# Values' bias moved into the output's bias, and the copy of the values moved from VectorE to ScalarE

## The chip, the cores and the metric

The kernel runs on one core of a Trainium2 chip. The metric is the device time of one execution in microseconds. TensorE, VectorE, ScalarE, GpSimd and SyncE each work through a program of their own and meet only at semaphores. In the profile they are PE (weight loads: PEld), DVE, ACT, POOL and SP.

## The reference: what is computed

```python
x = L0_attn_x                                  # (2, 2048, 128), float32
x = x + layernorm(attention(layernorm(x)))     # 16 heads of 64
x = x + layernorm(ffn(layernorm(x)))           # rank 32, 512 wide, gelu
# attention:
q, k, v = (einsum('bsd,dhk->bshk', x, W) + b for W, b in ((Wq, bq), (Wk, bk), (Wv, bv)))
attn = softmax(einsum('bqhd,bkhd->bhqk', q / 8, k))
out = einsum('bhqk,bkhd->bqhd', attn, v)
return einsum('bqhd,hdm->bqm', out, Wo) + bo
```

The rows of a softmax add up to 1. So the bias of the values passes through the attention unchanged, and the result equals attention without `bv` plus the constant row sum over h and k of `bv[h,k] * Wo[h,k,m]`.

## The kernel before

The 16 heads are taken as 8 pairs. A pair and one of the 2 batches make a **unit**; there are 16 units, numbered `u` from 0. A unit has 4 **quarters** `c` of 512 queries each, and a quarter has 16 steps, one for each tile of 128 keys. The program takes steps two at a time: a quarter has 8 **double steps** `d`, from 0 to 7, and the kernel has 512 of them, numbered `n`. "The sixth double step" is `d` = 5.

In one double step TensorE does, in this order:

- a pair of products for the row maxima of a later quarter (`max_pair`, L401), one for each head, each into one bank of the spare ring;
- the scores of two steps (L421, L424, L427, two matmuls each, twice), into two score buffers that ScalarE has filled beforehand with the negative maxima ("seeds");
- a second pair of products for maxima (L401);
- what is due in this double step: keys (`project_k`, L369), values (`project_v`, L387: two matmuls of 128 columns for each tile of 128 keys; in the trace every float32 matmul stands as two records, so four for a tile), queries (`project_q`, L378, at `d` = 2), output projection (`out_projection`, L487: 8 matmuls of 128 columns, 16 records, at `d` = 1);
- the products of probabilities and values of the two steps before (`values`, L442);
- at `d` = 3 the sums for the denominators (L454).

The **spare ring** is three banks of PSUM, r0, r1 and r2. The function `spare_banks` walks through the whole program in TensorE's order and gives each use the next bank of the three. `Pe.take` makes TensorE wait until the last user of a bank has been read. Each product for the maxima is reduced by VectorE (`dve_max`, L867).

ScalarE takes the exponentials of the two steps (`act_exp`, L691). In the last double step of a quarter (`d` = 7) its order is: exponential, seed, exponential, seed (`act_seed`, L681). A seed may be written only when the exponential that reads the same score buffer is done, and TensorE's scores of the first two steps of the next quarter wait for their own seed (`seed_done`). ScalarE also copies keys and queries out of PSUM with their biases, and copies the outputs of a quarter (`act_o`, L697).

VectorE does the maxima, four for a double step; the sums over groups of four probability tiles (`dve_part`, L903, at `d` = 3, 5, 6 and 1); the merge of these (`d` = 2); the addition of the output projection into `y_acc` (`dve_y`, L946); and the copy of the values with their bias added (`dve_v`, L858). GpSimd adds up the other part of the probabilities (`pool_add`, L1142), normalises the outputs (L935) and forms the low part of the keys (L1161). SyncE issues the DMAs.

The places of the projections are written out by hand in tables: `V_AT` maps a quarter and a double step of unit `u` to first tile and number of tiles of the values of unit `u + 1`. `FIRST_V_AT` is the same for unit 0. `OWN_V_AT` gives the values of unit 0 itself, in the first three double steps. In all there are 106 groups.

Of the kernel before, what the change touches and what calls it, by code (L numbers as in the profile page):

```python
# [47 lines left out]
V_AT = {(0, 7): (0, 2), (1, 7): (2, 2), (2, 4): (4, 2), (2, 7): (6, 2), (3, 0): (8, 3), (3, 4): (11, 3), (3, 7): (14, 2)}  # L48
# [5 lines left out]
WO_AT = 1  # L54

# [8 lines left out]
FIRST_V_AT = {(2, 7): (0, 4), (3, 0): (4, 4), (3, 4): (8, 4), (3, 7): (12, 4)}  # L64
# [51 lines left out]
def spare_banks():  # L116

    out = {}

    def use(*key):  # L120
        out[key] = f"r{len(out) % 3}"

    for n in range(DOUBLES):
        G, u, c, d = n // PER_CHUNK, n // (PER_CHUNK * NC), n // PER_CHUNK % NC, n % PER_CHUNK
        for st in (2 * n + LEAD, 2 * n + LEAD + 1):
            for h in range(2 if st < STEPS else 0):
                use("max", 2 * st + h)
        if keys_at(u, c, d):
            v, k = keys_at(u, c, d)
            use("K", v * NC + k)  # L130
        if values_at(u, c, d):
            v, t0, nt = values_at(u, c, d)
            use("V", v * T + t0)
        if d == Q_AT and G + 2 < CHUNKS:
            use("Q", G + 2)
        if projected_at(G, d) is not None:
            use("Wo", projected_at(G, d))
        if n in HEADS_AT:
            use("Wo0", HEADS_AT[n])
            use("Wo1", HEADS_AT[n])  # L140
        if n == CENTRE_AT:
            use("U")
        for g in ffn_at(n, XT):
            use("xT", g)
        for g in ffn_at(n, P_AT):
            use("p", g)
        if d == L_AT and 0 < G <= CHUNKS - COLUMN_CHUNKS:
            use("L", G - 1)
        if n in COLUMNS_AT:
            use("L", COLUMNS_AT[n])  # L150
    order = [("xT", 6), ("L", CHUNKS - 1), ("Wo0", CHUNKS - 1), ("Wo1", CHUNKS - 1), ("q", 0), ("p", 6), ("z", 0), ("q", 1), ("z", 1),
             ("q", 2), ("z", 2), ("q", 3), ("xT", 7), ("z", 3), ("p", 7), ("q", 4), ("z", 4), ("q", 5), ("z", 5), ("q", 6), ("z", 6),
             ("q", 7), ("z", 7)]
    for k, key in enumerate(order):
        out[key] = ("r0", "r1", "r2", "o")[k % 4]
    return out
# [5 lines left out]
def build(nc, x, Wq, bq, Wk, bk, Wv, bv, Wo, bo, U1, V1, b1, U2, V2, b2, out):  # L162
# [8 lines left out]
    bv_v = bv.rearrange("(i h) k -> i (h k)", h=2)  # L171

    ctx = ExitStack()
    with ctx:
# [12 lines left out]
        b_v = sb("b_v", [P, 2, P])  # L187
# [48 lines left out]
        def psum(name, shape):  # L236
# [14 lines left out]
            neg_max_done neg_rows_done""".split()  # L251
# [4 lines left out]
        W_DMA_N = 7 * 16  # L256
# [41 lines left out]
        def half(h):  # L298
            return slice(h * HD, (h + 1) * HD)

# [19 lines left out]
        class Pe:  # L320
# [4 lines left out]
            def take(self, name, kind, n):  # L325
# [171 lines left out]

            def centre(self):
# [46 lines left out]
        def pe_program(pe):  # L545
# [26 lines left out]
            for n in range(DOUBLES):  # L572
# [82 lines left out]
        def act_k_high(act, u, c):  # L655
# [5 lines left out]
            nc.scalar.activation(kd_hi[:, u % B, c * CH:(c + 1) * CH], key_diff[:], ACT.Copy).then_inc(s["kd_hi_done"], 1)  # L661

# [93 lines left out]
        def act_program(act):  # L756
# [16 lines left out]
            act_x(act, 4)  # L773
            act_x(act, 5)
# [8 lines left out]
            for n in range(DOUBLES):  # L783
# [6 lines left out]
                if last:  # L790
                    act_seed(act, 2 * n + 3)
                if keys_at(u, c, d):
# [60 lines left out]
        def dve_v(dve, u, t0, nt, name=None):  # L853
            at = u * T + t0
            dve.wait_ge(s["v_ps"], at + nt)
            if u >= 2 and t0 == 0:
                dve.wait_ge(s["pv_done"], (u - 1) * NC * T)
            nc.vector.tensor_tensor(v_sb[:, u % B, t0:t0 + nt, :],  # L858
                                    bank[name or SPARE["V", at]][:, 0:nt * P].rearrange("p (t n) -> p t n", t=nt),
                                    b_v[:, u // B % 2, :].unsqueeze(1).to_broadcast([P, nt, P]), ALU.add).then_inc(s["v_done"], nt)  # L860
# [76 lines left out]
        def dve_y(dve, G):  # L937
# [4 lines left out]
            if G < B * NC:  # L942
                dve.wait_ge(s["bo_in"], 16)
# [102 lines left out]
        def dve_program(dve):  # L1046
            for g in range(NG):
                dve_x_statistics(dve, g)
            for n in range(LEAD):
# [4 lines left out]
                if n == T:  # L1054
                    dve_v(dve, 0, 0, TC, FIRST_V_BANK)
            for n in range(DOUBLES):
# [18 lines left out]
                if values_at(u, c, d):  # L1075
                    dve_v(dve, *values_at(u, c, d))
# [132 lines left out]

        def pool_program(pool):  # L1210
# [33 lines left out]
            first_rstd(7)  # L1244
            for n in range(DOUBLES):
# [32 lines left out]
        def weights(queue, i):  # L1278
# [7 lines left out]
            for dst, src in ((w_qkv[:, j, 1, :], wk_v[i]), (b_qk[:, j, 1:2], bk_v[i].unsqueeze(1)),  # L1286
                             (w_qkv[:, j, 0, :], wq_v[i]), (b_qk[:, j, 0:1], bq_v[i].unsqueeze(1)),
                             (w_qkv[:, j, 2, :], wv_v[i]), (b_v[:, j, :], bv_v[i].partition_broadcast(P)),
# [22 lines left out]
        def sp_denom_back(sp, G):  # L1311
# [3 lines left out]
            if G >= 2:  # L1315
                sp.wait_ge(s["o_norm_done"], G - 1)
            for h in range(2):
# [97 lines left out]
```

## Time and profile before

| | us |
|---|---|
| device time, median of 3 runs | 2386.64 (2386.33 to 2387.66) |
| the profiled execution: its device time | 2388.58 |
| the profiled execution: span from first to last instruction | 2386.7 |
| PE busy in the span | 2348.6 (98%) |
| DVE busy | 2035.4 (85%) |
| ACT busy | 1415.4 (59%) |
| POOL busy | 2107.2 (88%) |
| granted TensorE clock, mean | 0.992 of full speed |

The span is 1.9 us shorter than the device time of the same execution. A timeline row gives start, duration, engine, line of the program, operation, what is written and read, and how many instructions were merged into the row; in brackets stands the idle time before and what ended it. The length of a double step is the distance between the first L421 of one double step and the first L421 of the next.

### The profile page before, as it was taken

Reading aid. Unit: us, or ns where it says so; the run is one execution under the profiler, and the core shown is the slowest. Engines: PE = TensorE matmul, PEld = TensorE weight load, DVE = VectorE, ACT = ScalarE, POOL = GpSimd, SP = SyncE. Lnnn points to the kernel's source line nnn. Section 1 sums busy time; section 2 is a strip of 40 time slices with the busy share of each in tenths; the row PEclk is TensorE's granted clock in tenths of the full one; section 3 lists DMA queues with packets and bytes.
Section 4 is the critical chain, followed back from the end, with each engine's and each line's share of the span. In section 5 each row is a group of like instructions: output and inputs, shape, how many; then the busy total and the mean of one; then the engine's idle time right before and its main releaser. Section 6 shows DMA issues by size and latency. Waiting matters only on the chain.

```text
span 2386.7 us, 43553 instructions
## 1 busy us (share of the span) xinstructions
PE 2348.6 (98%) x15628; PEld 1178.0 (49%) x15628; DVE 2035.4 (85%) x3208; ACT 1415.4 (59%) x1671; POOL 2107.2 (88%) x1206
## 2 busy tenths in 40 slices
PE   6999999999999999999999999999999999999998
PEld 3455454545445454454545445454544545444454
DVE  7888888888888888888888888888888888888877
ACT  5656556566565656656565655656656565655646
POOL 5888989888898989989888898989989888899986
PEclk8999999999999999999999999999999999999999
DMA  1100001000000000100001000100000000110101
GB/s 51 29 14 28 28 15 33 28 15 28 28 20 28 28 15 28 34 15 27 28 16 32 28 19 23 33 23 20 28 27 20 28 28 15 35 30 21 37 27 36
DMA packets 62969, 62.55 MB, mean 26 GB/s; under 512 B 28868, under 2 KB 46660, under 8 KB 62756
## 3 DMA queue, kind: packets, MB, share of 16 engines
q1 hardware_dynamic: 61748, 59.44, 8.5%
q8 instruction: 127, 2.08, 0.4%
q14 instruction: 86, 0.70, 0.1%
q10 hardware_dynamic: 1008, 0.33, 0.1%
HBM read 56.88 MB, written 2.61 MB: 25 GB/s over the span
## 4 chain that ended last, share of the span: by engine, by line
PE 94%; DVE 2%; POOL 1%; DMA 1%; ACT 1%; issue 1%; SPq 0%; POOLq 0%; DVEq 0%; ACTq 0%
PE o_ps L442 37%; PE spare_ps L401 14%; PE score_ps L421 10%; PE score_ps L427 10%; PE score_ps L424 10%; PE spare_ps L387 3%; PE spare_ps L487 3%; PE spare_ps L378 3%; PE spare_ps L369 3%; PE spare_ps L454 1%; DVE max_part L867 1%; POOL total L1142 1%; DMA m_all<-m_scratch 0%; DVE ln_stats L835 0%; PE spare_ps L467 0%
## 5 line engine op out<-in xcount | busy, mean ns | idle before, releaser
L1142 POOL TENSOR_TENSOR total<-total,probs 128x832 f32<-128x832 f32 (+1 forms) x896 | 1761.0, 1965 | 232.6 <-ACT probs L691 161.1
L867 DVE TENSOR_REDUCE max_part<-spare_ps 128x1 f32<-128x512 f32 x2027 | 1303.6, 685 | 295.3 <-PE spare_ps L401 276.7
L691 ACT ACTIVATE probs<-score_ps 128x1024 f32<-128x1024 f32 x1024 | 999.2, 1021 | 785.4 <-PE score_ps L427 784.2
L442 PE MATMUL o_ps<-probs,v_sb 128*64 128x512 f32 x4096 | 977.2, 598 | 0.0
L442 PEld LDWEIGHTS o_ps<-probs,v_sb 128*64 128x64 f32 x4096 | 268.3, 136 | 434.7 <-issue 282.5
L401 PE MATMUL spare_ps<-k_hi,q_hi 64*128 64x512 f32 x2027 | 466.2, 454 | 6.9 <-DVE max_part L867 3.2
L401 PEld LDWEIGHTS spare_ps<-k_hi,q_hi 64*128 64x128 f32 x2027 | 195.2, 184 | 436.8 <-issue 262.1
L421 PE MATMUL score_ps<-q_hi,kd_hi 64*128 64x512 f32 x2048 | 406.9, 393 | 0.9 <-ACT score_ps L681 0.9
L427 PE MATMUL score_ps<-q_hi,kd_lo 64*128 64x512 f32 x2048 | 405.2, 392 | 0.0
L424 PE MATMUL score_ps<-q_lo,kd_hi 64*128 64x512 f32 x2048 | 403.8, 390 | 0.0
L903 DVE TENSOR_REDUCE part_sum<-probs 128x192 f32<-128x768 f32 (+1 forms) x255 | 392.4, 1539 | 0.8 <-ACT probs L691 0.7
L427 PEld LDWEIGHTS score_ps<-q_hi,kd_lo 64*128 64x128 f32 x2048 | 193.2, 185 | 45.2
L424 PEld LDWEIGHTS score_ps<-q_lo,kd_hi 64*128 64x128 f32 x2048 | 193.2, 185 | 42.6
L421 PEld LDWEIGHTS score_ps<-q_hi,kd_hi 64*128 64x128 f32 x2048 | 193.6, 185 | 36.9 <-issue 7.3
L1142 POOL TENSOR_TENSOR total<-probs 128x832 f32<-128x832 f32 x64 | 125.8, 1966 | 14.9 <-ACT probs L691 14.8
L681 ACT ACTIVATE score_ps<-m_all 128x1024 f32<-128x1024 f32 x128 | 131.6, 1029 | 8.0 <-DMA m_all<-m_scratch 4.1
L912 DVE TENSOR_REDUCE total<-part_sum 128x192 f32<-128x768 f32 x64 | 96.9, 1515 | 0.0
L1161 POOL TENSOR_TENSOR kd_lo<-key_diff,kd_hi 128x512 fp32r<-128x512 f32 x64 | 81.7, 1277 | 0.7 <-ACT kd_hi L661 0.7
L387 PE MATMUL spare_ps<-w_qkv,xnT 128*64 128x128 f32 x1008 | 79.0, 285 | 0.4
L935 POOL TENSOR_TENSOR o_sb<-o_sb,denom 128x512 f32<-128x512 f32 x61 | 78.3, 1283 | 0.0
L703 ACT ACTIVATE denom<-spare_ps 128x256 f32<-128x256 f32 x61 | 23.5, 384 | 88.0 <-PE spare_ps L454 88.0
L387 PEld LDWEIGHTS spare_ps<-w_qkv,xnT 128*64 128x64 f32 x1008 | 53.6, 137 | 35.7 <-DVE max_part L867 34.6
(136 smaller groups left out, 1118.5 us busy)
## 6 DMA issues: line engine op xcount, KB each, us to landing
m_all<-m_scratch SPq DMA_DIRECT2D x64, 512.0 KB, 4.4
denom<-denom_scratch SPq DMA_DIRECT2D x122, 128.0 KB, 2.9
m_scratch<-neg_rows SPq DMA_DIRECT2D x256, 1.0 KB
y_acc<-in_L_attn_x SPq DMA_DIRECT2D x8, 256.0 KB, 6.6
key_f<-in_L_attn_x SPq DMA_DIRECT2D x8, 256.0 KB, 2.8
block_out<-probs SPq DMA_DIRECT2D x8, 256.0 KB, 2.3
denom_col<-denom SPq DMA_DIRECT2D x61, 4.0 KB
denom_scratch<-denom_col SPq DMA_DIRECT2D x61, 4.0 KB, 1.4
```

The lines of the kernel that those rows point to most:

```text
L387: last = nc.tensor.matmul(ps[half(k), t * P:(t + 1) * P], xnT[:, at0:at0 + HD], w_qkv[:, slot, 2, :], start=True, stop=True)
L401: last = nc.tensor.matmul(ps[h], q_hi[half(h), G % Q_RING, qt * P:(qt + 1) * P], k_hi[half(h), b, kc * CH:(kc + 1) * CH], start=True, stop ...
L421: nc.tensor.matmul(score_ps[j][:, h, :], kd_hi[half(h), b, keys], q_hi[half(h), G % Q_RING, :], start=False, stop=False, skip_group_check= ...
L424: nc.tensor.matmul(score_ps[j][:, h, :], kd_hi[half(h), b, keys], q_lo[half(h), G % Q_RING, :], start=False, stop=False, skip_group_check= ...
L427: last = nc.tensor.matmul(score_ps[j][:, h, :], kd_lo[half(h), b, keys], q_hi[half(h), G % Q_RING, :], start=False, stop=True, skip_group_ ...
L442: last = nc.tensor.matmul(o_ps[half(h), :], v_sb[:, b, kt, half(h)], probs[:, st % RING, h, :], start=(kt == 0), stop=(kt == T - 1))
L681: nc.scalar.activation(score_ps[st % 2][:], m_all[:], ACT.Copy).then_inc(s["seed_done"], 1)
L691: nc.scalar.activation(probs[:, st % RING], score_ps[st % 2][:], ACT.Exp, scale=SCALE).then_inc(s["exp_done"], 1)
L867: nc.vector.reduce_max(max_part[:, G % 2, h, qt, kc:kc + 1], bank[max_bank(n, h)], AX.X).then_inc(s["max_done"], 1)
L903: nc.vector.tensor_reduce(part_sum[:, k % (T // GROUP), 0:share(G)], probs[:, at:at + GROUP, 0, 0:share(G)].rearrange("p r n -> p n r"), A ...
L912: nc.vector.tensor_reduce(total[:, G % 2, 0, 0:share(G)], part_sum[:, 0:parts, 0:share(G)].rearrange("p g n -> p n g"), AX.X, ALU.add).the ...
L1142: nc.gpsimd.tensor_tensor(others(total[:, G % 2], G), so_far, others(probs[:, st % RING], G), ALU.add).then_inc(s["sum_done"], 1)
```

## The change

The values are projected without a bias. All sixteen tiles of a unit's values are projected in four groups of four tiles, one group at `d` = 5 of each quarter (before: seven groups of two or three tiles, at `d` = 7 of each quarter, `d` = 4 of the third, and `d` = 0 and 4 of the fourth). ScalarE copies each group (`act_v`), after the two exponentials of the double step; VectorE no longer does. The tables for unit 0 are changed too.

The constant row is computed once: two DMAs bring all of `Wo` into the `denom` buffers (unused at that time) and `bv` into a 128 x 8 tile; GpSimd multiplies and adds up over the 8 pairs; in double step 3 TensorE sums over partitions with a matrix of ones (two matmuls of 128 columns, one more use of the spare ring); VectorE adds the result to `bo`. The loads of `bv` with each pair's weights go away (8 DMAs). The first denominators' DMA waits for the read of the `denom` buffers, and the first additions into `y_acc` wait for the summed bias.

```diff
-V_AT = {(0, 7): (0, 2), (1, 7): (2, 2), (2, 4): (4, 2), (2, 7): (6, 2), (3, 0): (8, 3), (3, 4): (11, 3), (3, 7): (14, 2)}
+V_AT = {(0, 5): (0, 4), (1, 5): (4, 4), (2, 5): (8, 4), (3, 5): (12, 4)}
+BIAS_AT = 3
-FIRST_V_AT = {(2, 7): (0, 4), (3, 0): (4, 4), (3, 4): (8, 4), (3, 7): (12, 4)}
+FIRST_V_AT = {(1, 5): (0, 4), (2, 5): (4, 4), (3, 4): (8, 4), (3, 6): (12, 4)}
...
+            def bias(self):
+                self.pe.wait_ge(s["bias_scaled"], 4)
+                ps = self.take(SPARE["bias",], "bias", 0)
+                for k in range(2):
+                    last = nc.tensor.matmul(ps[half(k), 0:D], ones[:], bias_rows[:, 0, :], start=True, stop=True)
+                last.then_inc(s["bias_ps"], 1)
...
+        def act_v(act, u, t0, nt, name=None):
+            at = u * T + t0
+            act.wait_ge(s["v_ps"], at + nt)
+            if u >= 2 and t0 == 0:
+                act.wait_ge(s["pv_done"], (u - 1) * NC * T)
+            nc.scalar.activation(v_sb[:, u % B, t0:t0 + nt, :].rearrange("p t n -> p (t n)"), bank[name or SPARE["V", at]][:, 0:nt * P],
+                                 ACT.Copy).then_inc(s["v_done"], nt)
...
                 act_exp(act, 2 * n + 1)
                 if last:
                     act_seed(act, 2 * n + 3)
+                if values_at(u, c, d):
+                    act_v(act, *values_at(u, c, d))
                 if keys_at(u, c, d):
                     act_k(act, *keys_at(u, c, d))
...
             act_x(act, 4)
+            act_v(act, 0, 0, TC, FIRST_V_BANK)
             act_x(act, 5)
...
-        def dve_v(dve, u, t0, nt, name=None):
-            ...
-            nc.vector.tensor_tensor(v_sb[:, u % B, t0:t0 + nt, :],
-                                    bank[name or SPARE["V", at]][:, 0:nt * P].rearrange("p (t n) -> p t n", t=nt),
-                                    b_v[:, u // B % 2, :].unsqueeze(1).to_broadcast([P, nt, P]), ALU.add).then_inc(s["v_done"], nt)
+        def dve_bias(dve):
+            dve.wait_ge(s["bo_in"], 16)
+            dve.wait_ge(s["bias_ps"], 1)
+            nc.vector.tensor_tensor(bo_sb[:], bank[SPARE["bias",]][:, 0:D], bo_sb[:], ALU.add).then_inc(s["bias_done"], 1)
...
+        def pool_bias(pool):
+            pool.wait_ge(s["bias_in"], 32)
+            nc.gpsimd.tensor_tensor(bias_rows, bias_rows, b_v[:].unsqueeze(2).to_broadcast([P, PAIRS, D]), ALU.mult).then_inc(s["bias_scaled"], 1)
+            for k, count in enumerate((4, 2, 1)):
+                pool.wait_ge(s["bias_scaled"], k + 1)
+                nc.gpsimd.tensor_tensor(bias_rows[:, 0:count, :], bias_rows[:, 0:count, :], bias_rows[:, count:2 * count, :],
+                                        ALU.add).then_inc(s["bias_scaled"], 1)
...
             first_rstd(7)
+            pool_bias(pool)
...
             if G >= 2:
                 sp.wait_ge(s["o_norm_done"], G - 1)
+            elif G == 0:
+                sp.wait_ge(s["bias_ps"], 1)
...
             sp.dma_start(bo_sb[:], bo.partition_broadcast(P)).then_inc(s["bo_in"], 16)
+            sp.dma_start(bias_rows, wo_rows).then_inc(s["bias_in"], 16)
+            sp.dma_start(b_v[:], bv_v, allow_slow_non_contiguous=True).then_inc(s["bias_in"], 16)
             sp_m_out(sp, 0)
```

## Rows read from the trace of the kernel before

**Rows 1.** The page's first part: busy time of each engine, share of the span.

```profile
PE 2348.6 (98%) x15628; PEld 1178.0 (49%) x15628; DVE 2035.4 (85%) x3208; ACT 1415.4 (59%) x1671; POOL 2107.2 (88%) x1206
```

**Rows 2.** Waits: engine, line, releaser: total us, times, longest.

```profile
PEld spare_ps L401 <- DVE max_part L867: 154.5, 284, 2.1
PE score_ps L421 <- ACT score_ps L681: 0.9, 4, 0.3
```

**Rows 3.** TensorE's timeline in unit 6, double step 5 of quarter 0 onwards.

```profile
927.14 0.40 PE L421 MATMUL score_ps<-q_hi,kd_hi 64*128 64x512 f32 x2
...
931.05 0.40 PE L421 MATMUL score_ps<-q_hi,kd_hi 64*128 64x512 f32 x2
...
935.06 0.40 PE L421 MATMUL score_ps<-q_hi,kd_hi 64*128 64x512 f32 x2
...
936.94 0.66 PE L387 MATMUL spare_ps<-w_qkv,xnT 128*64 128x128 f32 x8
...
939.58 0.40 PE L421 MATMUL score_ps<-q_hi,kd_hi 64*128 64x512 f32 x2
...
940.29 0.39 PE L421 MATMUL score_ps<-q_hi,kd_hi 64*128 64x512 f32 x2
...
944.36 0.39 PE L421 MATMUL score_ps<-q_hi,kd_hi 64*128 64x512 f32 x2
...
946.07 1.09 PE L487 MATMUL spare_ps<-w_o,o_sb 128*64 128x128 f32 x16
...
949.15 0.40 PE L421 MATMUL score_ps<-q_hi,kd_hi 64*128 64x512 f32 x2
```

**Rows 4.** VectorE's timeline over the same double steps.

```profile
930.16 1.52 DVE L903 TENSOR_REDUCE part_sum<-probs 128x192 f32<-128x768 f32 x1
931.59 2.66 DVE L867 TENSOR_REDUCE max_part<-spare_ps 128x1 f32<-128x512 f32 x4
```

**Rows 5.** ScalarE's timeline over the same double steps.

```profile
929.87 0.63 ACT L661 ACTIVATE kd_hi<-key_diff 128x512 fp32r<-128x512 f32 x1
931.96 1.94 ACT L691 ACTIVATE probs<-score_ps 128x1024 f32<-128x1024 f32 x2 [1.46 <-PE score_ps L427]
...
937.98 1.01 ACT L691 ACTIVATE probs<-score_ps 128x1024 f32<-128x1024 f32 x1
939.02 1.03 ACT L681 ACTIVATE score_ps<-m_all 128x1024 f32<-128x1024 f32 x1
```

**Rows 6.** TensorE's timeline in unit 0, double step 7 of quarter 0 onwards.

```profile
79.22 0.40 PE L421 MATMUL score_ps<-q_hi,kd_hi 64*128 64x512 f32 x2
...
83.22 0.39 PE L421 MATMUL score_ps<-q_hi,kd_hi 64*128 64x512 f32 x2
...
84.27 0.50 PE L421 MATMUL score_ps<-q_hi,kd_hi 64*128 64x512 f32 x2 [0.19 <-ACT score_ps L681]
...
88.45 0.39 PE L421 MATMUL score_ps<-q_hi,kd_hi 64*128 64x512 f32 x2
```

**Rows 7.** ScalarE's timeline at the same place of unit 0.

```profile
83.19 1.03 ACT L681 ACTIVATE score_ps<-m_all 128x1024 f32<-128x1024 f32 x1
```

**Rows 8.** Groups of instructions by form: count, busy us, mean ns, idle before.

```profile
L697 ACT ACTIVATE o_sb<-o_ps 128x512 f32<-128x512 f32 x64 | 38.3, 599 | 50.0 <-PE o_ps L442 50.0
L935 POOL TENSOR_TENSOR o_sb<-o_sb,denom 128x512 f32<-128x512 f32 x61 | 78.3, 1283 | 0.0
```

**Rows 9.** The start-up, rows of the timeline of SP, PE and POOL.

```profile
38.74 1.59 SPq L1298 DMA_DIRECT2D m_scratch<-neg_rows  x4
...
40.53 0.80 PE L401 MATMUL score_ps<-k_hi,q_hi 64*128 64x512 f32 x2 [0.31 <-DVE v_sb L858]
...
51.46 1.95 POOL L1142 TENSOR_TENSOR total<-probs 128x832 f32<-128x832 f32 x1 [14.64 <-ACT probs L691]
```

**Rows 10.** DMA issues by tile: count, KB each, median us to landing.

```profile
y_acc<-in_L_attn_x SPq DMA_DIRECT2D x8, 256.0 KB, 6.6
b1c<-in_L_ffn_b SPq DMA_DIRECT2D x1, 2.0 KB, 2.4
```

More of the change, by code:

```diff
@@ L137, in spare_banks @@
             use("Wo", projected_at(G, d))
+        if n == BIAS_AT:
+            use("bias")
         if n in HEADS_AT:
@@ L170, in build @@
     bk_v = bk.rearrange("(i h) k -> i (h k)", h=2)
-    bv_v = bv.rearrange("(i h) k -> i (h k)", h=2)
+    bv_v = bv.rearrange("(i h) k -> (h k) i", h=2)
+    wo_rows = Wo.rearrange("(i h) k m -> (h k) i m", h=2)
     ctx = ExitStack()
@@ L186, in build @@
         b_qk = sb("b_qk", [P, 2, 2])
-        b_v = sb("b_v", [P, 2, P])
+        b_v = sb("b_v", [P, PAIRS])
         w_o = sb("w_o", [P, 2, D])
@@ L250, in build @@
             denom_copied col_dma recip_done scratch_dma recip_col_done y_half denom_dma o_copied o_norm_done wo_ps_ready y_done max_ready max_done
-            neg_max_done neg_rows_done""".split()
+            neg_max_done neg_rows_done bias_in bias_scaled bias_ps bias_done""".split()
         s = {n: ctx.enter_context(nc.semaphore(n)) for n in names}
@@ L255, in build @@
         m_dma = [s["m_dma0"], s["m_dma1"]]
-        W_DMA_N = 7 * 16
+        W_DMA_N = 6 * 16
         f_names = """v1_high v1_split f_low f_u1_ps f_u1 f_wst f_wmv f_wc f_ep1 f_nm1 f_ep2 f_ep3 ffn_w_in g_in0 g_in1 f_st1 f_mv1 f_rs1 f_t1 f_yn_late f_x1 f_x1_late f_st2 f_mv2
@@ L299, in half @@
             return slice(h * HD, (h + 1) * HD)
+        bias_rows = denom[:].rearrange("p h (i m) -> p (h i) m", m=D)
         FIRST_XT_BANK = ["o", "s10"] * 2 + ["o"] * 4
@@ L350, in take @@
                     pe.wait_ge(s["exp_done"], k + 1)
+                elif was == "bias":
+                    pe.wait_ge(s["bias_done"], 1)
                 elif was == "U":
@@ L589, in pe_program @@
                     me.head_projections(HEADS_AT[n])
+                if n == BIAS_AT:
+                    me.bias()
                 if n == CENTRE_AT:
@@ L851, in dve_x_statistics @@
             statistics(dve, [y_acc[:, g * TC + t, :] for t in range(TC)], g, s["stats_done"], s["mv_done"], g)
-        def dve_v(dve, u, t0, nt, name=None):
[L854 to L857, printed above, removed]
-            nc.vector.tensor_tensor(v_sb[:, u % B, t0:t0 + nt, :],
-                                    bank[name or SPARE["V", at]][:, 0:nt * P].rearrange("p (t n) -> p t n", t=nt),
-                                    b_v[:, u // B % 2, :].unsqueeze(1).to_broadcast([P, nt, P]), ALU.add).then_inc(s["v_done"], nt)
+        def dve_bias(dve):
+            dve.wait_ge(s["bo_in"], 16)
+            dve.wait_ge(s["bias_ps"], 1)
+            nc.vector.tensor_tensor(bo_sb[:], bank[SPARE["bias",]][:, 0:D], bo_sb[:], ALU.add).then_inc(s["bias_done"], 1)
         def dve_max(dve, n, h):
@@ L942, in dve_y @@
             if G < B * NC:
-                dve.wait_ge(s["bo_in"], 16)
+                dve.wait_ge(s["bias_done"], 1)
                 dve.wait_ge(s["xn_done"], TC * (g + 1))
@@ L1074, in dve_program @@
                     dve_neg_max(dve, G + 1)
-                if values_at(u, c, d):
-                    dve_v(dve, *values_at(u, c, d))
+                if n == BIAS_AT:
+                    dve_bias(dve)
                 if projected_at(G, d) is not None:
@@ L1287, in weights @@
                              (w_qkv[:, j, 0, :], wq_v[i]), (b_qk[:, j, 0:1], bq_v[i].unsqueeze(1)),
-                             (w_qkv[:, j, 2, :], wv_v[i]), (b_v[:, j, :], bv_v[i].partition_broadcast(P)),
+                             (w_qkv[:, j, 2, :], wv_v[i]),
                              (w_o[:, j, :], wo_v[i])):
```

2 lines of the change are left out of this document (removed).

## The prediction

> **What bounds the kernel now.** I read the page's first part first: PE is busy for 2348.6 of 2386.7 us, so the other engines count only where they make PE wait [rows 1]. Busy PE is not yet PE without a stall: PE's records run into each other, and a short wait shows mainly as idle time of the weight loads. So I next read the waits: weight loads of L401 stood 154.5 us behind VectorE's maxima, most of it harmless since PE was still working, and the wait for a seed is small, 0.9 us in four cases [rows 2]. Neither sum can be used as a price. The timeline gives prices: the distance between the first L421 of one double step and of the next. The bare one (`d` = 5, unit 6) is 931.05 - 927.14 = 3.91 us [rows 3]. Whatever a double step has above 3.91 is either projection or stall.
>
> **Price of the projection.** `d` = 1 has the output projection, 16 records of 128 columns (each float32 matmul of the program leaves two), and takes 949.15 - 944.36 = 4.79 us, 0.88 more than the bare one: 0.055 for a record [rows 3]. So two tiles of values (8 records) cost 0.44, three 0.66, four 0.88. A group has no price of its own in this: I take the same 1024 records to cost the same before and after, so that merging groups by itself gives nothing; `d` = 7 below bears it out.
>
> **VectorE's lag.** In `d` = 5 the sum over four tiles starts at 930.16 and takes 1.52, so the maxima of `d` = 6 can start only at 931.59 and run without a pause (four in 2.66) [rows 4]. The second L401 pair waits for one of them: `d` = 6 takes 935.06 - 931.05 = 4.01, a stall of 0.10. `d` = 6 has such a sum too, so `d` = 7 stalls again. With its 8 records of values it takes 4.52: 3.91 + 0.44 + 0.17 [rows 3]. After the change `d` = 5 has 0.88 of values on PE, longer than VectorE's part of the work (four maxima, a sum and a reciprocal). VectorE catches up, `d` = 6 becomes bare: -0.10 in each quarter. The sum in `d` = 6 then makes `d` = 7 stall by the 0.10 that `d` = 6 has now.
>
> **What the values in `d` = 7 hide.** This is the step on which the forecast turns. ScalarE's chain in `d` = 7 is exponential, seed, exponential, seed, without a pause: the second exponential starts at 937.98, the second seed at 939.02 and ends at 940.05. TensorE's second set of scores of the next quarter starts at 940.29 [rows 3, 5]. The chain starts from `d` = 7's own first scores (935.06), so it ends 4.99 later, however short the double step is. Unit 0 shows what happens with no values in `d` = 7, in two of its quarters. `d` = 7 takes 83.22 - 79.22 = 4.00; the second seed runs from 83.19 to 84.22; the second scores wait and start at 84.27, 5.05 after 79.22, where in unit 6 they start 0.71 after the first, which would be 83.93 [rows 6, 7]. The two double steps 7 and 0 (0 with keys in both cases) take 88.45 - 79.22 = 9.23 together. In unit 6, with two tiles of values in `d` = 7, they take 944.36 - 935.06 = 9.30 [rows 3]. So taking 0.44 of values out of `d` = 7 shortens the pair by 0.07: they lie almost wholly beside the seed, and PE waits instead. Before, this wait hardly occurs [rows 2]; after, it comes at every boundary between quarters of units 1 to 14, and at two more in unit 0. It appears as about 0.45 us in `d` = 0.
>
> **The sum for one of units 1 to 14.** `d` = 5: 4 x 0.88 = +3.52. `d` = 6: 4 x -0.10 = -0.40. Four pairs of `d` = 7 and 0: 4 x -0.07 = -0.28. Third quarter's `d` = 4: -0.44. Fourth quarter's `d` = 0: -0.66 (its pair is bound by the seed afterwards, as the others). Fourth quarter's `d` = 4: -0.66. Together +1.08, for fourteen units +15.1. Unit 0: two groups into `d` = 5 and one into `d` = 6, 2.64 + 0.08 (the values' bank waits for VectorE, as 0.17 against 0.10 above); two lags of 0.10 gone, -0.20; third `d` = 7 and fourth `d` = 0, which held four tiles each: a pair of 3.91 + 3.91 + 1.76 + 0.17 = 9.75 becomes 9.23 - 0.87 (keys: 4.78 - 3.91) = 8.36, -1.39; its fourth `d` = 7: -0.51. Together +0.6.
>
> **ScalarE's copies.** 64 copies of 128 x 512 out of PSUM, 0.60 each [rows 8]. In `d` = 5 the exponentials end at 929.87, then comes 0.63 of keys, then 1.46 idle before the next exponential [rows 5]; `d` = 5 becomes longer by 0.88. 0.60 fits in: 0. Were that cover missing, each copy would delay an exponential by up to 0.60, 33 us over 56 quarters; the rows have over 2 us. Queued behind it are the keys' high part and GpSimd's low part, needed a unit later. The bank is asked for again by the third L401 after it, 3 us after the copy. VectorE loses 106 additions (about 50 us of work), paid only as the 0.10 above.
>
> **Start and end.** GpSimd's four instructions on 1024, 512, 256 and 128 columns are, at 1.28 for 512 [rows 8], about 4.8 us, in an idle stretch of 14.64 before 51.46 [rows 9]: 0. Their DMAs are issued once the loads of `x` are; SP has nothing else until 38.74. Bounds for landing: 256 KB took 6.6, and 512 single numbers 2.4 [rows 10]; for 512 KB and 1024 numbers I take under 20 us, ready before GpSimd is free. The DMA of the first denominators waits for a matmul a whole quarter older. The eight loads of `bv` were awaited by nobody on the path. TensorE's bias product: four records, +0.2. Before, PE waited 0.31 for VectorE's first values at 40.53 [rows 9], on the chain through the maxima to the first scores: between 0 and -0.68 (a whole addition), I take -0.3. The tail keeps its order: 0. A shift of the ring by one bank changes no distance between uses.
>
> A page speaks of the new DMA. The Trainium skill, "DMA: Bandwidth & Descriptors", section "Rules for kernel authors", says that a pattern with a strided last dimension becomes a descriptor per element, and to avoid it. The transposed `bv` is such a pattern; the row of 512 numbers in 2.4 us says that here it is cheap, and the sum is the same by either while it lands before 36.
>
> **Result.** +15.1 + 0.6 + 0.2 - 0.3 = +15.6. Against the profiled execution: span 2386.7 to 2402.3, device time 2388.6 to 2404.2. The median of the runs is 1.9 below that execution, so 2386.6 + 15.6 = 2402.2 us.
>
> **Rivals.**
>
> *VectorE was the brake* (faster). If the next quarter's scores did not wait for the seed, for instance because ScalarE's chain moved forward, each of 56 boundaries would be 0.45 shorter, and two in unit 0: 15.6 - 26.1 = -10.5, time 2376. For it: the 154.5 us behind VectorE [rows 2]. Against it: rows 6 and 7; nothing in the change touches the order in `d` = 7. Chance 0.06. The Trainium skill, "Perfetto Trace Analysis", section "Optimization Strategies", would have one optimise those engines that keep the matmul engine waiting; by that rule VectorE's relief is the gain, and this is its outcome.
>
> *The lag stays in `d` = 6.* If VectorE is no earlier in `d` = 6, 56 x 0.10 come back: 2407.8. Against it: in `d` = 5 PE now takes 4.79, VectorE's work 4.4. Chance 0.10.
>
> *GpSimd's bias sum is late.* If the DMAs land after 46, every us more delays the exponentials and the first scores by one: 2403 to 2408. Chance 0.04.
>
> *The seed's wait is half hidden*, by shorter copies or an earlier first exponential: 28 x 0.45 less, 2389.6. Chance 0.04.
>
> **Chances.** Forecast 0.76. Its own error: 0.03 us in a price is 1.7 us over 56 quarters. The range, 2394 to 2409, takes in the lag and the late sum. What can be told from no change is about 0.2%, 4.8 us: faster 0.06, same 0.04, slower 0.90.
>
> **What would show it.** `d` = 5: 4.79; `d` = 6: 3.91; `d` = 7: 4.0 with no value matmuls; `d` = 0: 4.35 without keys and 5.2 with them; waits of L421 for the seed in some sixty places; a unit from 142.4 to 143.5. VectorE's busy time falls by about 50 us, ScalarE's rises by 38. It would be wrong if PE's L421 does not wait after `d` = 7, or `d` = 5 takes much over 4.8.

## The result, and the profile after

| | before | after |
|---|---|---|
| device time, median (6 runs each, same chip) | 2387.36 (2386.33 to 2390.54) | 2404.3 (2403.39 to 2405.86) |
| the profiled execution: device time | 2388.58 | 2403.39 |
| its span | 2386.7 | 2401.6 |

The ratio is 1.0072, 95% interval 1.0062 to 1.0082: 16.9 us slower. The forecast was 2402.2, or +15.6.

The page after: busy time of each engine [rows 1 before].

```profile
PE 2351.0 (98%) x15632; PEld 1170.3 (49%) x15632; DVE 2001.4 (83%) x3103; ACT 1455.5 (61%) x1735; POOL 2110.8 (88%) x1210
```

PE is as busy as before by its share, and DVE is busy for 34 us less. Neither number tells that the kernel got slower. The waits do (engine, line, releaser: total us, times, longest). L410 is the L401 of before, L430 is L421, and L708 is the seed, L681 before [rows 2].

```profile
PEld spare_ps L410 <- DVE max_part L893: 178.1, 269, 2.2
...
PEld score_ps L430 <- ACT score_ps L708: 36.9, 61, 0.8
...
PE score_ps L430 <- ACT score_ps L708: 8.0, 44, 0.3
```

The weight loads of the scores wait for the seed in 61 places, matmuls in 44; before it was 7 and 4 (3.6 and 0.9 us). Counted in the timeline, the second scores of a quarter start over 0.9 behind its first in 61 of 63 new quarters, before in 4. The 36.9 us and PE's 8.0 are again no price: PE works on while a weight load waits. The price is read from the timeline. This is TensorE's in unit 6, from `d` = 5 of quarter 0 on, the place of [rows 3] (L396 is L387 of before).

```profile
931.16 0.39 PE L430 MATMUL score_ps<-q_hi,kd_hi 64*128 64x512 f32 x2
...
932.86 1.09 PE L396 MATMUL spare_ps<-w_qkv,xnT 128*64 128x128 f32 x16
...
935.94 0.40 PE L430 MATMUL score_ps<-q_hi,kd_hi 64*128 64x512 f32 x2
...
939.85 0.40 PE L430 MATMUL score_ps<-q_hi,kd_hi 64*128 64x512 f32 x2
...
943.86 0.39 PE L430 MATMUL score_ps<-q_hi,kd_hi 64*128 64x512 f32 x2
...
944.91 0.51 PE L430 MATMUL score_ps<-q_hi,kd_hi 64*128 64x512 f32 x2 [0.19 <-ACT score_ps L708]
945.25 0.39 PE L433 MATMUL score_ps<-q_lo,kd_hi 64*128 64x512 f32 x2
...
946.93 1.89 PE L451 MATMUL o_ps<-probs,v_sb 128*64 128x512 f32 x8
948.75 0.50 PE L410 MATMUL spare_ps<-k_hi,q_hi 64*128 64x512 f32 x2
949.08 0.39 PE L430 MATMUL score_ps<-q_hi,kd_hi 64*128 64x512 f32 x2
```

The first scores stand 4.78, 3.91, 4.01 and 5.22 us apart (`d` = 5, 6, 7, 0). The second scores of the new quarter start 1.05 after its first, where 0.71 was enough before, and the row behind them follows after 0.34 (944.91 to 945.25), where rows without a wait stand 0.23 apart: 0.34 and 0.1 make the 0.44 that `d` = 0 is longer. The pair of 7 and 0 takes 949.08 - 939.85 = 9.23. ScalarE and VectorE at the same place [rows 5, 4]:

```profile
932.06 1.94 ACT L718 ACTIVATE probs<-score_ps 128x1024 f32<-128x1024 f32 x2 [1.06 <-PE score_ps L436]
934.05 0.60 ACT L687 ACTIVATE v_sb<-spare_ps 128x512 f32<-128x512 f32 x1
...
936.84 1.94 ACT L718 ACTIVATE probs<-score_ps 128x1024 f32<-128x1024 f32 x2 [1.67 <-PE score_ps L436]
...
942.79 1.01 ACT L718 ACTIVATE probs<-score_ps 128x1024 f32<-128x1024 f32 x1
943.83 1.03 ACT L708 ACTIVATE score_ps<-m_all 128x1024 f32<-128x1024 f32 x1
```

```profile
936.15 1.29 DVE L893 TENSOR_REDUCE max_part<-spare_ps 128x1 f32<-128x512 f32 x2 [0.44 <-PE spare_ps L410]
...
938.96 1.52 DVE L929 TENSOR_REDUCE part_sum<-probs 128x192 f32<-128x768 f32 x1
940.40 2.65 DVE L893 TENSOR_REDUCE max_part<-spare_ps 128x1 f32<-128x512 f32 x4
```

The copy of the values (L687) runs between the exponentials and the next idle time of 1.67. The second seed ends at 944.86 and PE's scores start at 944.91. VectorE is idle before the maxima of `d` = 6, since TensorE is the later one there; in `d` = 7 it runs four in a row and TensorE waits.

Over the units 2 to 13 the mean lengths of the double steps are these (worked out from the first scores of every double step of both traces; c0 is quarter 0):

```
             d0   d1   d2   d3   d4   d5   d6   d7    sum
before c0  3.94 4.79 4.78 4.48 4.77 3.91 4.02 4.52  35.22
after  c0  4.35 4.79 4.78 4.48 4.76 4.79 3.91 4.02  35.87
before c1  4.80 4.79 4.77 4.48 4.77 3.91 4.02 4.52  36.06
after  c1  5.22 4.78 4.77 4.49 4.77 4.79 3.91 4.02  36.75
before c2  4.77 4.78 4.77 4.48 4.35 3.91 3.97 4.53  35.56
after  c2  5.23 4.78 4.77 4.48 3.91 4.79 3.92 4.03  35.92
before c3  4.57 4.79 4.78 4.49 4.56 3.91 4.01 4.52  35.64
after  c3  4.35 4.78 4.78 4.48 3.91 4.79 3.92 4.02  35.04
```

A unit of this table went from 142.5 to 143.6, +1.10. Over units 1 to 14 it is +15.5 in all. Unit 15 takes 0.8 more (0.64 of it in one double step, `n` = 488, 6.47 to 7.11), what follows it 0.3 more, unit 0 as long as before, and the first scores come 1.7 earlier: 15.5 + 0.8 + 0.3 - 1.7 = 14.9, the difference of the spans. The start was not foreseen like this. The clock differs there as well: TensorE's granted share of full speed in 32 to 40 us and 40 to 48 us of both executions (columns: busy us of PE, PEld, DVE, ACT, POOL with counts, PEclk, DMA share, GB/s). Before:

```profile
32.00:40.00 8.00, 6.13 (x24) 3.41 (x24) 7.93 (x16) 6.39 (x16) 4.34 (x9) 0.70 0.01 2
40.00:48.00 8.00, 5.37 (x20) 2.83 (x20) 6.75 (x12) 3.17 (x4) 0.00 (x0) 0.50 0.22 66
```

After:

```profile
32.00:40.00 8.00, 5.35 (x30) 2.94 (x28) 7.93 (x16) 7.44 (x19) 7.44 (x11) 1.00 0.02 4
40.00:48.00 8.00, 4.30 (x21) 2.91 (x21) 6.42 (x11) 3.18 (x4) 1.34 (x3) 0.71 0.20 66
```

1.00 is 2.4 GHz for the whole stretch, 0.50 is 1.2 GHz. The execution after had the higher level for all of 32 to 40 us and for some of the next stretch; the one before had lost it in a part of the first stretch and for all of the second.

### The profile page after: what moved, and what is told of

It reads as the page before. It is cut to its first block, busy times and chain, and to the rows that moved or that the text cites. A ratio compares the mean times of both kernels' runs of the same rounds, so it can differ in the third digit from the quotient of the medians.

```text
span 2401.6 us, 43479 instructions
## 1 busy us (share of the span) xinstructions
PE 2351.0 (98%) x15632; PEld 1170.3 (49%) x15632; DVE 2001.4 (83%) x3103; ACT 1455.5 (61%) x1735; POOL 2110.8 (88%) x1210
## 3 DMA queue, kind: packets, MB, share of 16 engines
HBM read 56.88 MB, written 2.61 MB: 25 GB/s over the span
## 4 chain that ended last, share of the span: by engine, by line
PE 89%; ACT 6%; DVE 2%; POOL 1%; issue 1%; DMA 1%; SPq 0%; POOLq 0%; ACTq 0%; DVEq 0%
PE o_ps L451 35%; PE spare_ps L410 13%; PE score_ps L430 10%; PE score_ps L436 9%; PE score_ps L433 9%; ACT probs L718 3%; PE spare_ps L396 3%; ACT score_ps L708 3%; PE spare_ps L496 3%; PE spare_ps L387 3%; PE spare_ps L378 3%; PE spare_ps L463 1%; DVE max_part L893 1%; POOL total L1166 1%; DMA m_all<-m_scratch 0%
## 5 line engine op out<-in xcount | busy, mean ns | idle before, releaser
L410 PE MATMUL spare_ps<-k_hi,q_hi 64*128 64x512 f32 x2027 | 460.2, 449 | 8.5 <-DVE max_part L893 4.6
L430 PE MATMUL score_ps<-q_hi,kd_hi 64*128 64x512 f32 x2048 | 412.7, 399 | 10.3 <-ACT score_ps L708 8.0
L410 PEld LDWEIGHTS spare_ps<-k_hi,q_hi 64*128 64x128 f32 x2027 | 193.0, 184 | 428.3 <-issue 227.7
L430 PEld LDWEIGHTS score_ps<-q_hi,kd_hi 64*128 64x128 f32 x2048 | 193.8, 186 | 65.4 <-ACT score_ps L708 36.9
L708 ACT ACTIVATE score_ps<-m_all 128x1024 f32<-128x1024 f32 x128 | 131.6, 1029 | 8.6 <-DMA m_all<-m_scratch 4.6
L396 PE MATMUL spare_ps<-w_qkv,xnT 128*64 128x128 f32 x1008 | 69.5, 280 | 0.1
L387 PE MATMUL spare_ps<-xnT,w_qkv 128*64 128x512 f32 x252 | 68.8, 625 | 0.0
```

Of the source, the lines that this page charges most:

```text
L387: last = nc.tensor.matmul(ps[half(h), :], w_qkv[:, slot, 0, half(h)], xnT[:, cols], start=True, stop=True)
L396: last = nc.tensor.matmul(ps[half(k), t * P:(t + 1) * P], xnT[:, at0:at0 + HD], w_qkv[:, slot, 2, :], start=True, stop=True)
L410: last = nc.tensor.matmul(ps[h], q_hi[half(h), G % Q_RING, qt * P:(qt + 1) * P], k_hi[half(h), b, kc * CH:(kc + 1) * CH], start=True, stop ...
L430: nc.tensor.matmul(score_ps[j][:, h, :], kd_hi[half(h), b, keys], q_hi[half(h), G % Q_RING, :], start=False, stop=False, skip_group_check= ...
L708: nc.scalar.activation(score_ps[st % 2][:], m_all[:], ACT.Copy).then_inc(s["seed_done"], 1)
```

## Experiments

Two theories stood against each other. **Places:** the matmuls of the values lay beside ScalarE's seed in `d` = 7, they lie in `d` = 5 now, and TensorE waits at each boundary instead. **Parts:** the copies on ScalarE, the bias path or VectorE's new slack move the time. All edits are to the kernel after, unless another is named. Intervals are of the ratio to the kernel before on the same chip.

### The old places, everything else new

```diff
-V_AT = {(0, 5): (0, 4), (1, 5): (4, 4), (2, 5): (8, 4), (3, 5): (12, 4)}
+V_AT = {(0, 7): (0, 2), (1, 7): (2, 2), (2, 4): (4, 2), (2, 7): (6, 2), (3, 0): (8, 3), (3, 4): (11, 3), (3, 7): (14, 2)}
```
(and `FIRST_V_AT` as before)

> The kernel after with the old tables of places (V_AT and FIRST_V_AT of before): bias through the output and copies on ScalarE, but groups of 2 and 3 tiles in d = 7, 4 and 0. Seed theory: the places are the whole cause, so 2387 within 1.5 us; d = 6 keeps 4.01 and d = 7 keeps 4.52. Rival (the bias sum, ScalarE's copies or the missing additions on VectorE matter): 2393 or more, or 2381 or less.

Measured: 2386.66 against 2386.43, ratio 0.9999 (0.9990 to 1.0008). `d` = 6 and `d` = 7 are back at 4.01 and 4.52. So the places are the whole loss. The bias path, ScalarE's copies and 105 additions fewer on VectorE together, in these places, are worth nothing that can be measured: the interval leaves some 2 us either way. The weight loads' waits for VectorE's maxima stand at 154.8 us in this run, as before (154.5), though the additions are gone.

### The copy back on VectorE, in the new places

```diff
+        def dve_v(dve, u, t0, nt, name=None):
...
+            nc.vector.tensor_copy(v_sb[...], bank[...]).then_inc(s["v_done"], nt)
```
(called in `d` = 5; ScalarE's call in the quarters' loop is gone)

> The kernel after, but in the main loop VectorE copies the groups of four tiles (a plain copy, 128 x 512 out of PSUM) in d = 5. Seed theory: still about 2404 (2403 to 2408): VectorE has some 5.1 us of work in d = 5 against 4.79 and starts d = 6 at most 0.4 late, which cost nothing or 0.05 a quarter; the engine of the copy is nearly indifferent. Rival (VectorE is the brake, its relief is worth 50 us of busy time in part): 2415 or more. Rival (ScalarE's copies delay the exponentials): 2395 or less.

Measured: 2403.91 against 2386.43, ratio 1.0069 (1.0054 to 1.0084), with all double steps within 0.02 of after. Which engine copies in `d` = 5 makes no difference.

### The seed's wait filled by a new order, after and before

TensorE does the first `values` product between the two sets of scores of a new quarter, while ScalarE writes the second seed. The same edit in both kernels:

```diff
                 me.scores(2 * n)
+                if n and d == 0:
+                    me.values(2 * n - 2)
                 me.scores(2 * n + 1)
...
-                if n:
+                if n and d:
                     me.values(2 * n - 2)
+                if n:
                     me.values(2 * n - 1)
```

> The kernel after, with one move in TensorE's program: in the first double step of a quarter the values' products of the older step stand between the two sets of scores instead of behind both. Nothing else. Seed theory (TensorE idles about 0.45 us at each of some 60 boundaries of quarters until the second seed is written): 0.93 us of other work now stands in that wait, so d = 0 falls from 4.35 and 5.22 to 3.92 and 4.78, a unit from 143.6 to 141.8, the time from 2404.3 to about 2378. Rival (the time went into the copies on ScalarE, or into larger groups of values): the order of these products is indifferent, the time stays within 2 us of 2404.

> The kernel before with the same move in TensorE's program. Seed theory: with values in d = 7 the second seed comes just in time, so there is nothing to fill but the two boundaries of unit 0: -0.9 us and a few tenths, 2385.5 to 2387.5. Rival (splitting the values' products is in itself a gain of the size seen in the kernel after): 2387 falls to about 2362.

Measured: in the kernel after 2399.0 (ratio to before 1.0049, 1.0034 to 1.0064), 5.3 less than 2404.3; in the kernel before 2408.22 (1.0089, 1.0072 to 1.0106), 21.8 more. Both expectations missed by about 20 us, in the same direction. TensorE's timeline with the order changed in the kernel before, at `d` = 0 of quarter 1, where no seed was waited for:

```profile
946.62 0.39 PE L421 MATMUL score_ps<-q_hi,kd_hi 64*128 64x512 f32 x2
...
947.08 0.39 PE L427 MATMUL score_ps<-q_hi,kd_lo 64*128 64x512 f32 x2
947.41 1.08 PE L442 MATMUL o_ps<-probs,v_sb 128*64 128x512 f32 x4
948.42 0.50 PE L421 MATMUL score_ps<-q_hi,kd_hi 64*128 64x512 f32 x2
948.75 0.40 PE L424 MATMUL score_ps<-q_lo,kd_hi 64*128 64x512 f32 x2
...
950.45 1.03 PE L442 MATMUL o_ps<-probs,v_sb 128*64 128x512 f32 x4
951.41 0.50 PE L401 MATMUL spare_ps<-k_hi,q_hi 64*128 64x512 f32 x2
951.75 0.40 PE L421 MATMUL score_ps<-q_hi,kd_hi 64*128 64x512 f32 x2
```

The double step takes 5.13, 0.33 more than before (4.80), with the same matmuls and no wait. From one row of score matmuls to the next it is 0.23 (946.62 to 947.08 is two rows). From L427 to the products it is 0.33 (947.08 to 947.41), and from L421 to L424 behind the switch back 0.33 again (948.42 to 948.75): 0.1 each. The products themselves are 0.215 for a record: from their start to the next matmul eight take 1.82 (946.93 to 948.75 in the kernel after) and four 0.96 (950.45 to 951.41), which leaves 0.10 for going back. In the extra visit four take 1.01 (947.41 to 948.42), so 0.15. The extra visit from the scores to the products of the values costs 0.1 + 0.15 + 0.1, in all 0.35: 21.8 us over 63 boundaries.

What in the visit costs this was not taken apart. Two things change with it: the operands (fp32r and one record for each matmul, against float32 and two) and the use of the array (64 rows onto 128 columns, against 128 onto 64). The last 0.1 needs neither, since it also follows a plain wait for the seed (944.91 to 945.25 above).

The difference of the two effects of one edit, 21.8 + 5.3 = 27.1 us, is what the late seed is worth, if the visit costs the same in both kernels. Of the 61 late places the kernel before has 4 as well, so it is 0.48 for each of the other 57. The double steps `d` = 0 of units 2 to 13 give it without start and end: the edit makes them 0.34 longer before and 0.09 shorter after, together 0.43. The forecast had 0.45.

### The wait put into the kernel before

If late seeds alone make the loss, a late seed must cost the old kernel as much. ScalarE gets one instruction more in the chain of `d` = 7 of the kernel before, first one of a single column ahead of the first seed:

```diff
                 if last:
+                    nc.scalar.activation(extra[:], minus_half[:, 0:1], ACT.Copy)
                     act_seed(act, 2 * n + 2)
```

> The kernel before, with one ScalarE instruction more (a copy of one column, about 0.2 us) between the first exponential and the first seed in d = 7 of each quarter. Seed theory: before, the second seed has 0.07 us in hand, so 0.13 us show at each of 56 boundaries and 0.2 at two: +7.7 us, 2395. Rival (ScalarE, busy for 59% of the span, has room there): 2387 to 2388.

Measured: 2387.6 against 2387.51, ratio 0.9998 (0.9989 to 1.0007). ScalarE's timeline in `d` = 7:

```profile
935.22 1.03 ACT L692 ACTIVATE probs<-score_ps 128x1024 f32<-128x1024 f32 x1 [2.11 <-PE score_ps L428]
936.14 0.19 ACT L789 ACTIVATE extra<-minus_half 128x1 f32<-128x1 f32 x1
936.28 1.03 ACT L682 ACTIVATE score_ps<-m_all 128x1024 f32<-128x1024 f32 x1
937.24 1.01 ACT L692 ACTIVATE probs<-score_ps 128x1024 f32<-128x1024 f32 x1
```

The seed starts 1.06 after the exponential, with the extra instruction or without (940.90 - 939.84 in the next experiment, which has none there). The extra one depends on nothing, begins before the exponential's record ends (936.14 against 936.25), and does not move the seed. So this run delayed nothing and tested nothing, and its expectation (2395) missed. The next one copies 256 columns between the first seed and the second exponential:

```diff
                     act_seed(act, 2 * n + 2)
+                    nc.scalar.activation(extra[:], m_all[:, 0, 0:256], ACT.Copy)
```

> The kernel before, with one ScalarE copy of 128 x 256 more in d = 7 of each quarter, between the first seed and the second exponential (such a copy takes 0.38 us alone; behind another instruction some 0.3). Its result is used by nobody. The instruction of one column tried before this fitted into a gap of the chain and tested nothing; this one can't. Seed theory: the chain to the second seed ends 0.3 to 0.38 later and had 0.07 in hand, so 0.23 to 0.31 show at each of 56 boundaries and a little more at two: +13 to +18 us over the kernel before, 2400 to 2406. Rival (ScalarE, busy for 59% of the span, has room): 2387 to 2388.

Measured: 2401.31 against 2386.78, ratio 1.0060 (1.0043 to 1.0076): +14.5. ScalarE in `d` = 7 of unit 6, whose first scores are at 938.94:

```profile
939.84 1.02 ACT L692 ACTIVATE probs<-score_ps 128x1024 f32<-128x1024 f32 x1 [2.09 <-PE score_ps L428]
940.90 1.03 ACT L682 ACTIVATE score_ps<-m_all 128x1024 f32<-128x1024 f32 x1
941.86 0.40 ACT L790 ACTIVATE extra<-m_all 128x256 f32<-128x256 f32 x1
942.17 1.00 ACT L692 ACTIVATE probs<-score_ps 128x1024 f32<-128x1024 f32 x1
943.20 1.03 ACT L682 ACTIVATE score_ps<-m_all 128x1024 f32<-128x1024 f32 x1
```

and TensorE at the boundary:

```profile
943.47 0.39 PE L422 MATMUL score_ps<-q_hi,kd_hi 64*128 64x512 f32 x2
...
944.29 0.50 PE L422 MATMUL score_ps<-q_hi,kd_hi 64*128 64x512 f32 x2
...
948.47 0.39 PE L422 MATMUL score_ps<-q_hi,kd_hi 64*128 64x512 f32 x2
```

The second seed ends at 944.23, 5.29 behind the first scores of `d` = 7 instead of 4.99, and the scores follow at 944.29. The pair takes 948.47 - 938.94 = 9.53: 9.23 and the 0.30 that the chain became longer. The matmuls of the values are all still in `d` = 7. A pair is thus as long as TensorE's work or as ScalarE's chain (plus 4.2), whichever is more; before they were within 0.1 of each other.

### Other fillers and other places

**Maxima instead of products between the scores** (no switch to float32):

```diff
+                if d == 0 and 2 * n + LEAD < STEPS:
+                    me.max_pair(2 * n + LEAD + 1)
                 me.scores(2 * n + 1)
```

> The kernel after, with the second pair of products for the maxima between the two sets of scores in d = 0, beside the wait for the seed. They are matmuls of the same kind as the scores, so TensorE does not change between kinds of matmul once more, which cost 0.35 us at each place when the values' products were put there. Seed theory: 0.23 us of work goes into a wait of 0.35, and the second product must wait for VectorE's reduction that ends at 0.9: d = 0 gets shorter by 0.2 to 0.34, 12 to 20 us in all, 2384 to 2392. Rival (TensorE has no wait there): 2404.

Measured: 2406.83 against 2386.78, ratio 1.0079 (1.0064 to 1.0094), nothing gained; a miss. TensorE's timeline shows why:

```profile
944.95 0.39 PE L430 MATMUL score_ps<-q_hi,kd_hi 64*128 64x512 f32 x2
...
945.99 0.50 PE L410 MATMUL spare_ps<-k_hi,q_hi 64*128 64x512 f32 x2 [0.18 <-DVE max_part L895]
946.30 0.43 PE L430 MATMUL score_ps<-q_hi,kd_hi 64*128 64x512 f32 x2
```

The pair starts 1.04 behind the first scores, because its bank of the spare ring is still with VectorE. The wait for the bank takes the place of the wait for the seed.

**All four tiles in the last double step**, `V_AT = {(0, 7): (0, 4), (1, 7): (4, 4), (2, 7): (8, 4), (3, 7): (12, 4)}`:

> The kernel after with all four tiles of each quarter in d = 7. Seed theory: d = 5 loses 0.88, the lag of 0.10 comes back in d = 6, the pair of d = 7 and 0 grows from 8.37 to 8.88 since only 0.44 of the 0.88 fit beside the seed: -0.27 a quarter, 2404.3 - 15 = 2389. Rival (the place is indifferent, size and engine matter): 2404.

Measured: 2389.27 against 2387.51, ratio 1.0006 (0.9997 to 1.0015). `d` = 7 is 4.96, `d` = 0 is 3.91 and 4.77, `d` = 6 has its lag of 0.10 again.

**Two in the sixth, two in the last**, `V_AT = {(0, 5): (0, 2), (0, 7): (2, 2), ..., (3, 5): (12, 2), (3, 7): (14, 2)}`:

> The kernel after with each quarter's four tiles split: two in d = 5 and two in d = 7. Seed theory: the two in d = 7 lie beside the seed (pair of d = 7 and 0 from 8.37 to 8.44 us without keys), the two left in d = 5 cost 0.44 and still let VectorE catch up: -1.48 us a unit, 2404.3 - 20.7 = 2383.6, that is 3 to 4 us faster than before. Rival (more and smaller groups cost by themselves, or four tiles at once are the gain): 2404 or slower.

Measured: 2385.26 against 2387.51, ratio 0.9987 (0.9978 to 0.9997). `d` = 5, 6 and 7 take 4.35, 3.92 and 4.53, `d` = 0 is 3.93 and 4.77. It beats the kernel before by 2 us, a tenth of a per cent, where 3 to 4 were expected. Two tiles are enough in `d` = 7 to cover the seed, and two are enough in `d` = 5 to let VectorE catch up.

**Two in the sixth, two in the seventh, and the new order of the products of values on it:**

> The move in TensorE's order of the first of these experiments, and the four tiles of a quarter split into two in d = 5 and two in d = 6. Seed theory: no wait for the seed as there; two tiles in d = 5 and in d = 6 give VectorE 4.35 us in each for its 4.3 to 4.4 us of work, so d = 7 loses its stall of 0.10 too: about 2372, 15 us faster than before. Rival (VectorE's lag is not what makes d = 7 4.01): 2378, as the move alone.

Measured: 2394.04 against 2387.51, ratio 1.0027 (1.0017 to 1.0037); missed by 22 us, what 63 extra visits to the products cost. Its `d` = 5, 6, 7 are 4.34, 4.34 and 3.91: values in `d` = 6 take the lag out of `d` = 7.

**On top of the half-and-half version, VectorE's third sum moved** from `d` = 6 to `d` = 7, so that no lag is left:

```diff
-PART_AT = {3: 0, 5: 1, 6: 2, 1: -1}
+PART_AT = {3: 0, 5: 1, 7: 2, 1: -1}
```

> The split into two tiles in d = 5 and two in d = 7, and VectorE's third sum over four tiles moved from d = 6 to d = 7. Theory of VectorE's lag: d = 7 of 4.52 holds 0.17 of stall from the sum in d = 6; it falls to about 4.36, and then the seed ends the pair: 8.37 instead of 8.45 us without keys, 0.08 x 56 = 4.5 us less than the split alone, 2381. Rival (the lag is not the sum's, or it moves into d = 0): 2385 or more.

Measured: 2385.04 against 2386.78, ratio 0.9990 (0.9981 to 1.0000); less than expected. `d` = 7 fell from 4.52 to 4.36, but `d` = 0 rose to 4.04 and 4.90, since the pair is now held by the seed; and the last unit lost 2.8 us (`n` = 488: 6.65 to 10.22). Giving that unit its old place:

```diff
+END_PART_AT = {3: 0, 5: 1, 6: 2, 1: -1}
...
-                part_at = LAST_PART_AT if G == CHUNKS - 1 else PART_AT
+                part_at = LAST_PART_AT if G == CHUNKS - 1 else END_PART_AT if G >= CHUNKS - NC else PART_AT
```

> The kernel with two tiles in d = 5 and two in d = 7 and VectorE's third sum in d = 7, but in the last unit the sum stays in d = 6, where VectorE also has the feed-forward part's work. The move gave 0.18 us in each of units 1 to 14 and cost 2.8 us in the last unit. Theory: the cost is the last unit's alone, so 2385.0 - 2.8 = 2382, some 5 us (0.2%) faster than the kernel before. Rival (the last unit's loss is chance from execution to execution): 2385.

Measured: 2381.67 against 2386.82, ratio 0.9978 (0.9969 to 0.9987), 5.2 us faster than the kernel before (0.2%) and the best of all. The reason given for it is borne out in part only. In its trace `n` = 488 is 8.80, still well above 6.65, and unit 15 with what follows takes 201.0, against 202.4 with the sum moved in all units and 199.6 with the split alone: only half of the 2.8 came back. Between these two traces the first scores come 1.6 earlier as well. TensorE in unit 6, `d` = 7 and `d` = 0 (L431 and L397 are L430 and L396 of after):

```profile
931.19 0.40 PE L431 MATMUL score_ps<-q_hi,kd_hi 64*128 64x512 f32 x2
...
932.89 0.66 PE L397 MATMUL spare_ps<-w_qkv,xnT 128*64 128x128 f32 x8
...
935.53 0.40 PE L431 MATMUL score_ps<-q_hi,kd_hi 64*128 64x512 f32 x2
936.23 0.50 PE L431 MATMUL score_ps<-q_hi,kd_hi 64*128 64x512 f32 x2
940.42 0.40 PE L431 MATMUL score_ps<-q_hi,kd_hi 64*128 64x512 f32 x2
```

`d` = 7 has two tiles of values and takes 4.34, with no lag. The second scores follow 5.04 after the first scores of `d` = 7: the pair is 940.42 - 931.19 = 9.23, the same as in the kernel after, but with 0.44 of values inside.

## Why the prediction was right, step by step

- **Price of the projection** (0.88 for four tiles): `d` = 5 is 4.79, and merging groups gave nothing. The term of +3.52 is 4 x 0.88 from the table.
- **VectorE's lag** (-0.10 in `d` = 6, kept in `d` = 7): 4.02, 4.02, 3.97 and 4.01 became 3.91 or 3.92, and `d` = 7 without values is 4.02. The runs with two tiles in `d` = 5 and with the sum moved show the same cause from two other sides.
- **What the values in `d` = 7 hide** (the pair of 7 and 0 falls from 9.30 by 0.07 alone): it takes 9.23. This was read from a single place in unit 0 [rows 6, 7] and held at 56 others. The opposite effects of one edit in the two kernels give 0.43 to 0.48 for each late seed, and the run with a longer chain gave +14.5 in the kernel before. "VectorE was the brake" fell with the run in the old places: all of VectorE's relief is there, and the time is 0.9999 of before. The Trainium skill, "Perfetto Trace Analysis", section "Optimization Strategies", says to optimise the engines that block the critical path while TensorE idles. The runs agree with it only as to what truly blocks: 154.5 us of waits stood behind VectorE, and relieving it bought nothing, nor did it shorten these waits (154.8); the 0.9 us behind the seed hid the chain that decided.
- **The sum for a unit:** +1.08 forecast, +1.10 measured, +15.1 and +15.5 over fourteen. Unit 0: the double steps that the values left or came to, with the pair that reaches into unit 1, are +0.69 (+0.6 forecast); 0.56 of this stands in unit 1's count, and the rest is taken back by the faster clock in unit 0's first two double steps (-0.33).
- **ScalarE's copies and the bias path:** 0 and 0. GpSimd's four instructions took 1.90 and 2.61 us from 36.91 on (4.8 forecast), and GpSimd then stood idle for 8.27. The transposed load of `bv` landed 5.8 us behind its issue at 8.79. TensorE's bias product made its double step 0.22 longer (0.2 forecast).
- **Start-up, mis-sized:** -0.3 forecast, -1.7 between the two traces. The ten profiled executions with the new start-up have the first scores at 45.65 to 46.47 (seven) and at 47.32 to 47.48 (three); the four with the old one have them at 46.81 to 46.86 (three) and at 47.53. So the same start-up varies by more than the change moves it. It goes with the granted clock from 20 to 46 us: this is 0.95 in the execution after and 0.73 in the one before. Two others with the new start-up have 0.73 as well, and their first scores come at 47.32 and 47.48, against 47.53 with the old one. So most of the 1.7 goes with the clock. How much is the change was not told apart: at 0.83 the new start-up is 0.3 to 0.5 earlier (46.28 and 46.47 against 46.81), but the one at 0.80 is 0.6 later (47.43) than the old ones at 0.78 and 0.79.
- **The end, put at 0:** unit 15 and what follows cost 1.1, 0.64 of it in the double step `n` = 488. There the second pair of products for maxima waits for VectorE's work for the feed-forward part. Before, after, and with the sum moved in all units:

```profile
2227.70 0.51 PE L401 MATMUL spare_ps<-k_hi,q_hi 64*128 64x512 f32 x2 [1.71 <-DVE kd_lo L1007]
2242.25 0.50 PE L410 MATMUL spare_ps<-k_hi,q_hi 64*128 64x512 f32 x2 [2.01 <-DVE kd_lo L1033]
2223.77 0.80 PE L410 MATMUL spare_ps<-k_hi,q_hi 64*128 64x512 f32 x2 [3.97 <-DVE kd_lo L1033]
```

The pair starts 3.25 behind the first scores before and 3.89 after, which is the 0.64. VectorE is that much later because the instruction ahead (L1005, L1031 after), the same in both, took 0.96 and 1.59; why it did was not taken apart. The clock has a part in the longer cases: in the ten traces whose granted clock is 1.00 in this double step it takes 5.36 to 7.14, in the four with 0.80 to 0.83 behind the wait it takes 8.32 to 10.22. One of these four has the old places (8.32), so the length of the end is not set by the places alone. Unit 15 with what follows takes 196.9 to 199.0 in the four traces of the kernel before and its variants, and 197.6 to 202.4 in the ten others.
- **Span and median:** the profiled executions differ by 14.8, the medians by 16.9: the one before was 1.2 above its median, the one after 0.9 below. The forecast's 15.6 lies between them. That the errors at the start (-1.4) and at the end (+1.1) nearly cancel between the two traces is luck; the sum over units 1 to 14 is not.
- **VectorE's busy time** was to fall by 50 and fell by 34. Its 106 additions (49.0 us) are gone and one for the bias came. Busy time is a union of records, not a sum, and records without a pause between them overlap by 0.08: four maxima of 0.685 count 2.65, two count 1.29. Summed up, VectorE's records fell by 47.5 us, and their overlap fell by 13.5 (182.5 to 169.0), since there are fewer such seams: 2043 after, 2201 before. ScalarE's busy time rose by 40 (38 forecast).

## What to carry to other kernels

Work on the bounding engine is free where that engine would otherwise wait for another engine's fixed chain. Before moving it, compare the two lengths at its old place: if they are near each other, the move turns cover into a wait, however small the wait in the profile of before. Fill such a place with just enough work to reach the end of the chain, and put the rest where a lagging engine can catch up; that split is in all three runs here that beat the kernel before, by 0.1 to 0.2%.

## What the runs showed of the hardware

- An extra visit of TensorE from score matmuls (fp32r, 64 rows onto 128 columns) to products of the values (float32, 128 rows onto 64 columns) and back costs about 0.35 us: 21.8 us for 63 in the kernel before, with no wait and the same matmuls. Whether the number format or the shape costs it was not tested. It turned three expected gains into losses or less.
- Behind a wait of TensorE for a seed, the next row of score matmuls followed after 0.34 us instead of 0.23.
- A one-column instruction of ScalarE that depends on nothing cost 0 between two dependent ones, whose starts were 1.06 apart either way. A copy of 256 columns, 0.40 long, delayed what followed by 0.30.
- With one and the same start-up the granted clock from 20 to 46 us was between 0.73 and 0.96 in ten executions, and the first scores came between 45.65 and 47.48.
- In `n` = 488 TensorE waits once for VectorE. The granted clock of this double step was 0.80 to 0.83 in four traces (waits of 1.70, 2.39, 2.49 and 3.97). In the ten others it was 1.00, with waits of 0.23 to 2.31.
